# A recommendation tower on one core: the upper norm moved to the front of its step, and the last block's dense part computed in step 2

## The reference

```
x = layer_norm(dense @ Wd.T)                     # 512 x 128
y = layer_norm(einsum('bnd,ed->bne', e, Ws))     # 26 rows of 128 a sample
y = layer_norm(einsum('bne,pn->bep', y, Wsi))    # mixed to 32 rows
T = concat([x, y])                               # 33 rows of 128 a sample
Z = T @ T.T, lower triangle                      # 528 numbers a sample
z = layer_norm(Zflat @ Wl.T)[:, :384]            # the linear layer and the upper norm
h = relu([z, dense] @ W_top1 + b_top1)           # 384 + 256 -> 512
h = relu(h @ W_top2 + b_top2);  out = h @ W_top3
```

## Time and profile before

| | us |
|---|---|
| median of 3 runs | 183.28 |
| lowest, highest | 182.54, 187.37 |
| the profiled execution | 184.72 |
| its span, first to last instruction | 182.9 |
| PE busy | 148.9 (81%) |
| DVE busy | 117.3 (64%) |
| POOL busy | 105.0 (57%) |
| ACT busy | 85.9 (47%) |

### The profile page before, as it was taken

How to read it: one execution, slowest core, us unless ns; L and a number is a source line. 1 busy time by engine, 2 the same in 40 slices (tenths; PEclk the granted TensorE clock), 3 DMA queues, 4 the chain that set the end, 5 groups by cost and what they waited for, 6 DMA issues and landing times.

```text
span 182.9 us, 4658 instructions
## 1 busy us (share of the span) xinstructions
PE 148.9 (81%) x1865; PEld 105.9 (58%) x1865; DVE 117.3 (64%) x279; ACT 85.9 (47%) x229; POOL 105.0 (57%) x108
## 2 busy tenths in 40 slices
PE   0474584658994979968896999999699999998995
PEld 0363262444452558635566977765398865596674
DVE  3799508794959999992969069968942898600000
ACT  3001324572634776752655256638604764522262
POOL 2778778787878787778777877788774000000000
PEclk9998869995899999999997899999969999999999
DMA  5714241325186633321255313212452102422000
GB/s 128 220 24 110 50 135 35 82 27 195 34 249 127 80 63 44 60 54 27 53 76 71 48 28 56 56 29 57 68 78 41 34 0 48 61 36 34 0 4 0
DMA packets 38520, 12.01 MB, mean 66 GB/s; under 512 B 34113, under 2 KB 35265, under 8 KB 38498
## 3 DMA queue, kind: packets, MB, share of 16 engines
q1 hardware_dynamic: 33586, 8.24, 20.2%
q0 software_dynamic: 3328, 3.41, 10.8%
q10 hardware_dynamic: 1584, 0.05, 0.5%
HBM read 9.46 MB, written 2.23 MB: 64 GB/s over the span
## 4 chain that ended last, share of the span: by engine, by line
POOL 36%; PE 34%; issue 14%; ACT 6%; DMA 5%; DVE 3%; SPq 1%; ACTq 0%
POOL rows L302 36%; PE pV L341 4%; PE pU L381 4%; PE pU L408 4%; PE pU L422 3%; PE pT L351 3%; PE pA L325 2%; PE pU L434 2%; PE pA L381 2%; PE pZ L364 2%; DMA zr<-zscr 1%; DMA rows<-in_tables,idx 1%; PE pA L318 1%; DMA idx_in<-in_index 1%; ACT ujunk L615 1%
## 5 line engine op out<-in xcount | busy, mean ns | idle before, releaser
L302 POOL DMA_INDIRECT rows<-in_tables,idx x104 | 104.7, 1007 | 34.3 <-issue 31.4
L756 DVE TENSOR_TENSOR prod<-pA,rows 128x384 f32<-128x384 f32 (+1 forms) x16 | 9.4, 591 | 28.8 <-PE pA L325 28.8
L780 DVE TENSOR_TENSOR t<-pT,bias 128x512 f32<-128x512 f32 x32 | 20.6, 684 | 4.3 <-PE pT L351 4.3
L584 ACT ACTIVATE t<-t 128x512 f32<-128x512 f32 x32 | 19.5, 629 | 7.4 <-DVE t L780 7.1
L795 DVE TENSOR_TENSOR T<-t,trs 128x512 f32<-128x512 f32 x32 | 22.2, 694 | 1.1
L318 PE MATMUL pA<-const,rows 128*128 128x128 f32 x52 | 9.0, 288 | 15.8 <-DMA rows<-in_tables,idx 15.8
L341 PE MATMUL pV<-wexp,srow 128*64 128x192 f32 (+4 forms) x256 | 21.4, 313 | 0.0
L786 DVE TENSOR_REDUCE tss<-t 128x16 f32<-128x512 f32 x32 | 20.4, 677 | 0.1
L325 PE MATMUL pA<-gbd,rowsT 128*128 128x128 f32 x104 | 17.5, 311 | 3.6 <-ACT rowsT L567 3.5
L364 PEld LDWEIGHTS pZ<-T 128*32 128x32 f32 x1024 | 12.2, 112 | 12.3 <-issue 9.8
L341 PEld LDWEIGHTS pV<-wexp,srow 128*64 128x64 f32 x256 | 16.4, 145 | 4.9 <-issue 2.7
(11 more groups left out here) (153 smaller groups left out, 214.0 us busy)
## 6 DMA issues: line engine op xcount, KB each, us to landing
zscr<-zs SPq DMA_DIRECT2D x16, 128.0 KB
rows<-in_tables,idx POOLq DMA_INDIRECT x104, 2.5
wl_sb<-in_wl SPq DMA_DIRECT2D x5, 256.0 KB, 2.9
w_sb<-in_w SPq DMA_DIRECT2D x5, 256.0 KB
dense_sb<-in_dense_t SPq DMA_DIRECT2D x1, 512.0 KB, 4.7
w_sb<-in_w SPq DMA_DIRECT2D x1, 512.0 KB, 4.5
zr<-zscr SPq DMA_DIRECT2D x3, 96.0 KB
const<-in_consts SPq DMA_DIRECT2D x1, 263.0 KB, 3.2
```

Of the source, the lines that this page charges most:

```text
L302: pool.indirect_dma_start(out=rows[:, j, h * D:(h + 1) * D], out_offset=None, in_=tables, in_offset=bass.IndirectOffsetOnAxis(ap=idx[:, 2 ...
L584: a.activation(t2[:, h], t1[:, n % 2, h], ACT.Square).then_inc(t_sq, 1)
L780: v.tensor_tensor(t1[:, n % 2, h], pT[h][:].rearrange("p (a b) -> p a b", b=PJ), bias[:].unsqueeze(1).to_broadcast([P, US, PJ]), ALU.add). ...
```

## The change

Six things move. (1) On DVE the inverse of the upper norm comes ahead of `row_variance` in steps 9 and 13; on ACT `upper_scaled` comes ahead of `mixed`, and `upper_turned` ahead of `interactions`; on PE `turn` comes ahead of `interact`. (2) In every step DVE's `scaled_rows` comes between the two halves of `biased`. (3) The dense part of hidden layer 1 of the last block is computed in step 2 (`dense_ahead`), copied to `hd` by ACT in step 3, and added by DVE at the end (`hidden_sum`), from where `relu1` reads. (4) The weights for it are loaded ahead of the linear layer's, whose loads shift by up to one step; SP is done with its weight loads one step sooner. (5) In step 16 and behind it, PE's `embed(15)` comes ahead of block 2's second product, and `interact(15)` ahead of its last two. (6) ACT's `interactions(15)` comes ahead of block 2's norm.

```diff
+        hd = sb("hd", [P, H1])
+        hs = sb("hs", [P, H1])
...
+            sp.wait_ge(r_done, 1)
+            for c in range(USED // P, (USED + DENSE) // P):
+                first = P * c + UO - USED
+                sp.dma_start(w1_sb[:, c, :], w1[first:first + P, :]).then_inc(ld_wd1, 16)
             for j in range(NL):
-                if j % 2 == 0:
-
-                    sp.wait_ge(r_done, 1 + j // 2)
+                if j % 2 == 1:
+                    sp.wait_ge(r_done, 2 + j // 2)
                 sp.dma_start(wl_sb[:, j, :], wl[:, j, :]).then_inc(ld_wl[j], 16)
-            for c in range((USED + DENSE) // P):
-                if c % 3 == 0:
-                    sp.wait_ge(r_done, 4 + c // 3)
-                first = P * c if P * c < USED else P * c + UO - USED
-                sp.dma_start(w1_sb[:, c, :], w1[first:first + P, :]).then_inc(ld_w1, 16)
+            sp.wait_ge(r_done, 4)
+            for c in range(USED // P):
+                sp.dma_start(w1_sb[:, c, :], w1[P * c:P * (c + 1), :]).then_inc(ld_w1, 16)
...
+            def dense_ahead():
+
+                pe.wait_ge(ld_wd1, 16 * (NK - USED // P))
+                pe.wait_ge(xsum_sb, 1)
+                for m in range(H1 // P):
+                    for c in range(USED // P, NK):
+                        got = mm(pU[:, P * m:P * (m + 1)], w1_sb[:, c, P * m:P * (m + 1)],
+                                 dense_sb[:, c - USED // P, P * LAST:P * (LAST + 1)], start=c == USED // P, stop=c == NK - 1)
+                got.then_inc(hd_done, 1)
...
             def hidden1_dense(k):
...
-                if k == LAST:
-                    pe.wait_ge(zs_sb, NU)
-                    pe.wait_ge(u_sb, LAST)
...
             def hidden1(k, part=range(USED // P)):
                 pe.wait_ge(zT_sb, k + 1)
                 if k == LAST:
+                    pe.wait_ge(zs_sb, NU)
+                    pe.wait_ge(t1_sb, 2 * NU)
                     for m in range(H1 // P):
                         for c in range(USED // P):
                             got = mm(hidden_part(k, m), w1g[:, c, P * m:P * (m + 1)], znT[:, c, :],
-                                     start=False, stop=c == USED // P - 1, skip_group_check=True)
+                                     start=c == 0, stop=c == USED // P - 1)
...
             def s_rows(part):
                 if part[0] == 0:
                     pe.wait_ge(beye_ready, 1)
-                    pe.wait_ge(xsum_sb, 1)
+                    pe.wait_ge(hd_sb, 1)
...
                 if (k := block_at(n, TOP)) is not None:
                     hidden1(k, [1, 2])
-                if n == NU:
-                    upper(LAST - 1, [1])
                 if n:
                     embed(n - 1)
                 if n == 0:
                     x_sums()
+                if (k := block_at(n, MLP)) is not None:
+                    turn(k)
                 if (k := block_at(n, ANS)) is not None:
                     answer(k)
                 if n >= 2:
                     interact(n - 2)
+                if n == 2:
+                    dense_ahead()
...
                 if (k := block_at(n, MLP)) is not None:
-                    turn(k)
                     hidden1_dense(k)
                     hidden1(k, [0])
                 if n == NU - 1:
                     upper(LAST - 1, [0])
                 if n == NU:
-                    upper(LAST - 1, [2, 3, 4, 5])
+                    upper(LAST - 1, [1, 2, 3])
             interact(NU - 1)
+            upper(LAST - 1, [4, 5])
             hidden1_dense(LAST - 1)
             turn(LAST - 1)
-            hidden1_dense(LAST)
             hidden1(LAST - 1)
...
             def relu1(k):
                 for m in range(H1 // P):
-                    if m == 0 or k == LAST:
-                        act.wait_ge(h1_done, H1 // P * k + (m + 1 if k == LAST else H1 // P))
-                    a.activation(h1[:, m, :], hidden_part(k, m), ACT.Relu, bias=b1p[:, m:m + 1]).then_inc(h1_sb, 1)
+                    got = hidden_part(k, m)
+                    if k == LAST:
+                        act.wait_ge(hs_sb, m + 1)
+                        got = hs[:, P * m:P * (m + 1)]
+                    elif m == 0:
+                        act.wait_ge(h1_done, H1 // P * (k + 1))
+                    a.activation(h1[:, m, :], got, ACT.Relu, bias=b1p[:, m:m + 1]).then_inc(h1_sb, 1)
...
+                if (k := block_at(n, MLP)) is not None:
+                    upper_scaled(k)
                 if n:
                     mixed(n - 1)
-                if (k := block_at(n, MLP)) is not None:
-                    upper_scaled(k)
                 if (k := block_at(n, ANS)) is not None:
                     relu2(k)
+                if n == 3:
+                    act.wait_ge(hd_done, 1)
+                    a.copy(hd[:], pU[:]).then_inc(hd_sb, 1)
...
+                if (k := block_at(n, MLP)) is not None:
+                    upper_turned(k)
                 if n >= 2:
                     interactions(n - 2)
-                if (k := block_at(n, MLP)) is not None:
-                    upper_turned(k)
...
+            interactions(NU - 1)
             upper_norm(LAST - 1)
             upper_scaled(LAST - 1)
-            interactions(NU - 1)
             x_row(LAST)
             upper_turned(LAST - 1)
...
+            def hidden_sum():
+
+                for m in range(H1 // P):
+                    dve.wait_ge(h1_done, H1 // P * LAST + m + 1)
+                    v.tensor_tensor(hs[:, P * m:P * (m + 1)], hidden_part(LAST, m), hd[:, P * m:P * (m + 1)],
+                                    ALU.add).then_inc(hs_sb, 1)
...
             for n in range(NU + 1):
+                if (k := block_at(n, MLP)) is not None:
+                    upper_inverse(k)
                 if n < NU:
                     row_variance(n)
-                if (k := block_at(n, MLP)) is not None:
-                    upper_inverse(k)
                 if n:
-                    biased(n - 1)
+                    biased(n - 1, 0)
                 if n < NU:
                     scaled_rows(n)
                 if n:
+                    biased(n - 1, 1)
                     variances(n - 1)
                     normalised(n - 1)
...
             upper_inverse(LAST - 1)
             upper_inverse(LAST)
+            hidden_sum()
```

More of the change, by code:

```diff
@@ L186, in build @@
             sem, ["ld_index", "ld_const", "ld_cols", "ld_ws", "ld_gs", "ld_wsi"])
-        ld_dense, ld_wd, ld_wlx, ld_w1, ld_w2 = map(sem, ["ld_dense", "ld_wd", "ld_wlx", "ld_w1", "ld_w2"])
+        ld_dense, ld_wd, ld_wlx, ld_wd1, ld_w1, ld_w2 = map(sem, ["ld_dense", "ld_wd", "ld_wlx", "ld_wd1", "ld_w1", "ld_w2"])
         ld_wl = [sem(f"ld_wl{i}") for i in range(NL)]
@@ L196, in build @@
         w1_ready, b1_done, b1_ready = map(sem, ["w1_ready", "b1_done", "b1_ready"])
+        hd_done, hd_sb, hs_sb = map(sem, ["hd_done", "hd_sb", "hs_sb"])
         gathered = [sem(f"gathered{i}") for i in range(NU)]
@@ L408, in hidden1_dense @@
                         mm(hidden_part(k, m), w1_sb[:, c, P * m:P * (m + 1)], dense_sb[:, c - USED // P, P * k:P * (k + 1)],
-                           start=c == USED // P and (m == 0 or k == LAST), stop=False, skip_group_check=True)
+                           start=c == USED // P and m == 0, stop=False, skip_group_check=True)
             def hidden1(k, part=range(USED // P)):
@@ L474, in hidden_bias @@
             def hidden_bias():
-                pe.wait_ge(ld_w1, 16 * NK)
+                pe.wait_ge(ld_w1, 16 * (USED // P))
                 pe.wait_ge(w9_ready, 1)
@@ L773, in scaled_rows, with biased @@
                                 ers[:, 0:2 * count].unsqueeze(2).to_broadcast([P, 2 * count, D]), ALU.mult).then_inc(s_sb, 1)
-            def biased(n):
-                if n >= 2:
+            def biased(n, h):
+                if n >= 2 and h == 0:
                     dve.wait_ge(t_sb, 2 * (n - 1))
-                for h in range(2):
-                    dve.wait_ge(y_done, 2 * n + h + 1)
-                    v.tensor_tensor(t1[:, n % 2, h], pT[h][:].rearrange("p (a b) -> p a b", b=PJ),
-                                    bias[:].unsqueeze(1).to_broadcast([P, US, PJ]), ALU.add).then_inc(t1_sb, 1)
+                dve.wait_ge(y_done, 2 * n + h + 1)
+                v.tensor_tensor(t1[:, n % 2, h], pT[h][:].rearrange("p (a b) -> p a b", b=PJ),
+                                bias[:].unsqueeze(1).to_broadcast([P, US, PJ]), ALU.add).then_inc(t1_sb, 1)
             def variances(n):
@@ L834, in hidden_weights @@
             def hidden_weights():
-                dve.wait_ge(ld_w1, 16 * ((USED + DENSE) // P))
+                dve.wait_ge(ld_w1, 16 * (USED // P))
                 for c in range(USED // P):
```

## The result

| | before | changed |
|---|---|---|
| median, lowest, highest (us) | 183.62, 182.54, 187.37 (4 runs) | 186.73, 185.62, 187.74 (4 runs) |
| the profiled execution, its span | 184.72, 182.9 | 186.43, 184.5 |

The ratio is 1.0197, 95% interval 1.0122 to 1.0271: slower; the medians differ by 3.1 us where 3.3 were forecast. The comparisons leave out executions more than 1.5% above the fastest of their kernel, so a ratio can differ from the quotient of the medians.

A forecast was written before the change was run, and what follows sets the result against it. POOL's gathers were taken to bound the kernel until step 9, then PE and what it waits for. Terms 0.76 + 0.63 + 0.65 + 0.95 + 0.34 = 3.3 us on median 183.28 gave 186.6; range 182.4 to 189.0.

The forecast's parts named there:

- The front: Steps 9 and 13: znT 0.32 us earlier ahead of zs, 0.70 later by scaled_rows between biased's halves; net +0.38 each.
- un ahead of vsb: Step 13: with un first on ACT, vsb ends 0.7 to 0.8 us later, of which 0.63 reaches t1.
- rowsT: Steps 11 and 15: gram starts on ACT's rowsT, 0.38 and 0.27 us later; +0.65 taken.
- embed(15): Last unit's embed: waits for ACT's vsb, said to end at the same time as before; costed at nothing.
- The tail: Last block's linear layer, upper(3), waits for the last read issued on ACT's queue and starts 0.95 us later.
- The addition: At the end, relu1 of block 3 waits for a DVE addition: +0.34 us (0.2 to 0.5).
- The dense part ahead: Block 3's eight dense products, taken from the tail, give nothing there; in step 2 they cost nothing.
- The price of the lower clock: Steps 9 and 13: the eight dense products after PE's wait take 1.65 us more at the lower clock, each time.
- Rival B: Step 13 keeps the full clock: 3.3 - 1.65 = 1.7 us slower, 185.0 us; chance 0.22.
- rival D: Steps 9 and 13: znT comes before interact ends; waits and clock losses go, 6.1 us, capped at 3.5; 181.1; chance 0.08.
- The sum: Whole kernel: the terms add up to 3.3 us over the median 183.28, forecast 186.6 us.
- Rival C: Tail: a third stretch at 1.2 GHz, price 1.65 us, so 5.0 slower, 188.3 us; chance 0.15.

The follow-up runs named there:

- e6: Kernel before with DVE's inverse and PE's turn earlier and ACT's znT ahead of both squares in steps 9 and 13: 182.52 us, before 184.26, ratio 0.9968.
- e8: Changed kernel with scaled_rows behind both halves of biased, vsb ahead of un, znT ahead of both squares: 183.38 us, before 183.55, ratio 1.0002.
- e11: The changed kernel itself again, on another chip, 12 executions: 184.66 us, before 183.55, ratio 0.9999.
- e4: Kernel before with the new order of the tail alone, block 3's dense products staying in the tail: 184.31 us, before 182.90, ratio 1.0070.
- e5: Changed kernel with scaled_rows again behind both halves of biased, all else as changed: 184.06 us, before 184.26, ratio 1.0117.
- e3: Kernel before with the last block's dense part ahead in step 2, its loads and the addition alone: 184.00 us, before 182.90, ratio 1.0051.
- e2: Kernel before with the moves in steps 9 and 13 alone, znT still behind both squares: 183.58 us, before 182.90, ratio 1.0012.
- e9: Kernel before with six idle products in PE's wait of steps 9 and 13: 183.15 us, before 184.26, ratio 1.0042.
- the second set: The executions of e11, the changed kernel on another chip: median 184.66 us, before 183.55, ratio 0.9999.

## Why the prediction was right, and where it wasn't

**The front: right.** znT stayed behind both squares, and the split took what its place ahead of zs gave. The two steps lengthened by 0.28 and 0.32, where the prediction had 0.38 each and another 0.63 in step 13. e6 and e8 remove the cause, and the wait is gone. **un ahead of vsb: mis-sized.** 0.63 was forecast, and step 13 as a whole gave 0.32 rather than 1.01. Counted from the start of step 12, DVE was through with T 0.21 later (9.62, before 9.41), near the 0.3 forecast. But PE began step 13 0.49 later on the same count, of which it waited 0.34 for a gather, and that hid most of it: PE waited 0.24 for vsb, and embed came 0.18 later after the transposes. The prediction counted with no step behind step 9 that begins on a gather; this one did. In e11 it didn't, and embed came 0.35 later.

**rowsT: right** in place; 0.53 for 0.65. The 0.18 of step 11 came to nothing: the step as a whole was 0.06 shorter than before. **embed(15): missed.** I cost it at nothing. ACT's copy of vsb stands behind the same squares and deviations; 0.24.

**The tail: right in sign, wrong in its cause.** The reads on ACT's queue were to set the end with 0.95. They began at 165.10, the last issue ended at 166.21, and they were in before PE came at 168.02, so PE's order set it, with 0.28; the prediction's count of PE's own path had given nothing (166.7 for 166.76). The last read landed at most 2.4 us after its issue began, sooner than the 2.69 of SP's. The fixed cost of 2.0 us in the Trainium skill (DMA: Bandwidth & Descriptors, Anatomy of one DMA) would have given 0.26, near the 0.28, but only by luck: it too has PE wait for the read, and the section gives the figure for transfers that POOL issues, not for those of ACT's queue (these are of 8 KB each, not 4). The trace allows 2.0 without measuring it. e4 shows the same order at its full price, 1.1 from embed(15) on; e5, without the split and without block 3's dense products in that place, has 0.18 of the 0.28, and embed(15) comes 0.25 sooner there.

**The addition: right,** 0.35 for 0.34. **The dense part ahead: right,** e3 shows the 1.68 us wait that it leaves.

**The price of the lower clock: too high.** The prediction has 1.65 us for the eight products, 3.32 less the 1.67 of a window in the tail. In the same place they take 1.89 at full clock (e2, e9), so 1.43. Rival B's 185.0 and rival D's 6.1 stand on it. It isn't in the forecast itself, and both traces kept a lower clock in both steps.

**The sum: right, and partly by luck.** The terms come to 2.0 and the path in the trace to 2.4, less 0.8 that the gathers gave; the forecast was 3.3. The first set's medians differ by 3.1, the second's by 1.1. So the direction and the mechanism of the front are shown, and that the number was met in the first set isn't explained by the terms. The gathers' gain, 0.8 and 2.1 in the two traces at step 9 (the second beside another chip's before), wasn't forecast at all. Rival C, a third stretch at 1.2 GHz, did not show in the tail of either trace of the changed kernel, where the clock is 1.00 throughout. (Its counter-argument was weak: no wait in the tail of before is over 0.77.) What the executions of 186 to 189 us in the second set spend their time on stays open: none of them was profiled.

## What to carry to other kernels

An instruction moved ahead in an in-order list gains only if it passes the one that is waiting: znT had to pass the squares, not the copies of zs. Look for the last instruction ahead of the one that is waited for, on each engine. When one wait is removed, work out how far the next limit is (here the gathers, which took 1.2 and 1.3 us of the removed waits back) before counting the rest. A reordering that costs on one path may pay elsewhere, so try it in the stage whose limit it helps, and only there.

## What the runs showed of the hardware

A gather issued by POOL takes 0.94 us. If it begins inside one of DVE's 128x512 or 128x384 tensor products with both inputs in SBUF (L795, L771), it takes longer by about what is left of the product, up to 1.5 us (146 of 269 over 1.2), except in 21 cases where it began 0.01 to 0.04 us after the product: there it took 0.94 and a 128x512 product took 0.73 to 0.77 rather than 0.69. A gather that begins beside a DVE addition that reads PSUM, or beside a sum, is never over 1.1 (433 of them).

PE waits of 1.29 to 2.45 us before the eight dense products were followed by a lower clock in 8 of 16 steps, and the same products took 1.89 us at 1.00 and 3.3 to 3.6 at 0.50 to 0.55. With the wait filled or removed, none of 12 stretches fell.
